# Scores of a local attention: one matmul for each head on 64 rows of TensorE, in place of one for each pair of heads on 128 rows with zeros in the keys

## What is computed

```python
HEADS, DIM_HEAD, WINDOW, QK_SCALE = 16, 64, 32, 8.0
q, k, v = split(x @ Wqkv)              # each [b, 16 heads, n, 64]
q = rotary(l2norm(q) * qs); k = rotary_inv(l2norm(k) * ksc)
# every window of 32 queries sees its own 32 keys and the 32 before them
bk2, bv2 = look(bk), look(bv)          # [b, h, windows, 64, 64]
sim = einsum('bhwie,bhwje->bhwij', bq, bk2) * QK_SCALE
sim = where(mask, -finfo.max, sim)     # it < jb, it > jb + w, or before the sequence
out = einsum('bhwij,bhwje->bhwie', softmax(sim), bv2) @ Wo
```

## Time and profile before

| | |
|---|---|
| median of 3 runs | 4558.43 us |
| the profiled execution, its own time | 4560.67 us |
| its span | 4558.9 us |
| transformer part | from about 1260 us to the end |
| PE busy over the span | 4228.4 us (93%) |
| DVE, ACT, POOL busy | 3608.9, 3009.7, 2849.6 us |
| granted TensorE clock, mean | 0.956 |

### The profile page before, as it was taken

How to read it: one execution, slowest core, us unless ns; L and a number is a source line. 1 busy time by engine, 2 the same in 40 slices (tenths; PEclk the granted TensorE clock), 3 DMA queues, 4 the chain that set the end, 5 groups by cost and what they waited for, 6 DMA issues and landing times.

```text
span 4558.9 us, 86667 instructions
## 1 busy us (share of the span) xinstructions
PE 4228.4 (93%) x32672; PEld 2902.5 (64%) x32672; DVE 3608.9 (79%) x4102; ACT 3009.7 (66%) x4797; POOL 2849.6 (63%) x1551
## 2 busy tenths in 40 slices
PE   5888889888759999999999999999999999999998
PEld 2333333333347777777877777777777777777775
DVE  3888898889867888787887888788887888878784
ACT  5655555555347777777777777777777777777774
POOL 0555455555457677676776767766676666766662
PEclk8898898988869999999999999999999999999999
DMA  1000000000010110001100010000100011000001
GB/s 37 0 0 0 0 0 0 0 0 0 19 44 22 33 31 22 22 22 33 31 22 25 19 43 22 23 23 20 45 19 25 22 33 30 19 25 22 22 22 49
DMA packets 144208, 96.47 MB, mean 21 GB/s; under 512 B 11694, under 2 KB 136624, under 8 KB 142776
## 3 DMA queue, kind: packets, MB, share of 16 engines
q1 hardware_dynamic: 143800, 90.93, 6.5%
HBM read 74.02 MB, written 16.88 MB: 20 GB/s over the span
## 4 chain that ended last, share of the span: by engine, by line
PE 68%; issue 2%; ACT 1%; POOL 1%; DVE 1%; DMA 0%; SPq 0%; ACTq 0%; POOLq 0%; DVEq 0%
PE ps L860 15%; PE ps L780 12%; PE ps L846 9%; PE ps L791 8%; PE ps L818 8%; PE ps L885 5%; PE ps L828 4%; PE ps L898 3%; PE ps L807 2%; PE ps L867 1%; PE ps L873 1%; PE ps L799 1%; PE ps L763 0%; ACT sq L950 0%; ACT w_qk L920 0%
## 5 line engine op out<-in xcount | busy, mean ns | idle before, releaser
L1269 POOL TENSOR_TENSOR resid<-resid,rnorm 128x1024 f32<-128x1024 f32 x384 | 726.8, 1903 | 537.4 <-DVE rnorm L1094 537.4
L425 POOL TENSOR_TENSOR read<-state,c_row 128x1024 f32<-128x1024 f32 x256 | 598.4, 2356 | 619.6 <-DVE state L411 494.7
L1259 POOL TENSOR_TENSOR resid<-resid,sq 128x1024 f32<-128x1024 f32 x384 | 909.0, 2372 | 101.8 <-DVE resid L1122 101.8
L860 PE MATMUL ps<-mixed,w_vo 128*128 128x128 f32 x6144 | 722.5, 276 | 4.2 <-ACT hidden L1042 2.7
L860 PEld LDWEIGHTS ps<-mixed,w_vo 128*128 128x128 f32 x6144 | 701.0, 192 | 21.6 <-issue 21.6
L780 PE MATMUL ps<-w_qk,xs_parts 128*128 128x512 f32 x2304 | 638.5, 413 | 38.9 <-DVE resid L1122 13.3
L229 PE MATMUL mamba_ps<-read,ident 128*128 128x512 f32 x1024 | 569.5, 695 | 22.4 <-DVE xc L366 19.8
L1122 DVE TENSOR_TENSOR resid<-ps,rope_l 128x1024 f32<-128x1024 f32 x384 | 467.5, 1217 | 112.9 <-ACT sq L950 109.9
L950 ACT ACTIVATE sq<-ps 128x1024 f32<-128x1024 f32 x384 | 394.3, 1027 | 239.6 <-PE ps L780 232.9
L1109 DVE TENSOR_TENSOR sq<-ps,rope_l 128x1024 f32<-128x1024 f32 x384 | 467.2, 1217 | 78.5 <-ACT sq L950 75.9
L780 PEld LDWEIGHTS ps<-w_qk,xs_parts 128*128 128x128 f32 x2304 | 417.8, 192 | 156.8 <-issue 68.2
(11 more groups left out here) (140 smaller groups left out, 6908.9 us busy)
## 6 DMA issues: line engine op xcount, KB each, us to landing
x_rows<-row_scratch SPq DMA_DIRECT2D x384, 128.0 KB, 2.8
row_scratch<-rows SPq DMA_DIRECT2D x192, 64.0 KB, 2.2
w_stage<-w_qk_hbm SPq DMA_DIRECT2D x6, 1024.0 KB, 5.9
vo_stage<-w_v_hbm SPq DMA_DIRECT2D x6, 512.0 KB, 4.0
vo_stage<-w_o_hbm SPq DMA_DIRECT2D x6, 512.0 KB, 4.8
xn<-x_hbm SPq DMA_DIRECT2D x4, 512.0 KB, 5.4
kept<-resid SPq DMA_DIRECT2D x8, 256.0 KB, 3.1
resid<-kept SPq DMA_DIRECT2D x8, 256.0 KB, 4.3
```

Of the source, the lines that this page charges most:

```text
L425: pool.tensor_tensor(read[:, u % 4, :], state[:, u % 4, :], c_row[:, (u // 2) % 2, :], ALU.mult).then_inc(read_ready, 1)
L860: last = pe.matmul(bank[:, 0:P], w_vo[:, 2 * a + h, :], mixed[:, odd, a, h, :], start=a + h == 0, stop=a == PAIRS - 1 and h == 1)
L1259: pool.tensor_tensor(qk[:, tile % 2, cols], qk[:, tile % 2, cols], sq[:, 2 + part, :], ALU.add).then_inc(done[f"rotated{part}"], 1)
L1269: pool.tensor_tensor(heads, heads, norms, ALU.mult).then_inc(done[f"normed{part}"], 1)
```

## The change

The score product is made with one matmul for each head. Head h of the pair (h = 0, 1) stands on its own 64 rows (64h to 64h + 63) in `q_t` as before and now also in `k_t`, which loses its second copy and its zeros. Each matmul has 64 rows, 32 weight columns and 64 moving columns (32 in the first window of a sequence). The first heads of all pairs go to bank S, the second ones to bank S + 1, so probabilities now stand in the order of `head_at`, and `output` picks the folded weights to match. ACT copies keys with one instruction of 128 partitions in place of two of 64. The ring has three tiles, and all four `copy_heads` wait for the score of two tiles back. The clearing of `k_t` on POOL is gone. All four order tables are new, and `copy_folded` stands ahead of the next `copy_mixed` in place of behind the last one.

```diff
-K_RING = 2
+K_RING = 3
+def head_at(place):
+    return place % PAIRS * 2 + place // PAIRS
 PE_ORDER = [
-    (3, None, "gate0"), (1, 1, "head_turn1"), (2, 2, "mix0"), (2, 1, "output"), (1, 1, "head_turn0"), (2, 2, "mix1"),
+    (2, 0, "output"), (1, 0, "row_turn"), (1, 2, "project1"), (1, 1, "head_turn3"), (1, 1, "head_turn2"), (2, 1, "mix1"),
...
-LAST_GELU = 0
+LAST_GELU = 1
...
-        mixed = [x for x in pe[:at] if x[0] in ("mix0", "mix1")][-1]
         pe.insert(at, ("fold", l))
-        insert_after(act, (mixed[0].replace("mix", "copy_mixed"), mixed[1]), ("copy_folded", l))
+        later = {(name.replace("mix", "copy_mixed"), k) for name, k in pe[at + 1:] if name in ("mix0", "mix1")}
+        act.insert(next(i for i, x in enumerate(act) if x in later), ("copy_folded", l))
...
-    k_t = sb("k_t", [P, K_RING, PAIRS, 2, P])
+    k_t = sb("k_t", [P, K_RING, PAIRS, P])
...
                 for a in range(PAIRS):
                     for w in range(WINDOWS):
-                        own = k_t[:, tile % K_RING, a, :, w * WINDOW:(w + 1) * WINDOW]
-                        to = ps[w * WINDOW:(w + 1) * WINDOW, S + a // 4, (a % 4) * P:(a % 4 + 1) * P]
...
+                        for h in range(2):
+                            rows_h = slice(64 * h, 64 * h + 64)
+                            own = k_t[rows_h, tile % K_RING, a, w * WINDOW:(w + 1) * WINDOW]
+                            first = a * 2 * WINDOW
+                            if w == 0 and t % SEQ_TILES == 0:
+                                first, keys = first + WINDOW, own
+                            elif w:
+                                keys = k_t[rows_h, tile % K_RING, a, (w - 1) * WINDOW:(w + 1) * WINDOW]
+                            else:
+                                back = k_t[rows_h, (tile - 1) % K_RING, a, P - WINDOW:P].offset
+                                keys = bass.AP(own.tensor, back, [own.ap[0], (own.offset - back, 2), (1, WINDOW)])
+                            last = pe.matmul(ps[w * WINDOW:(w + 1) * WINDOW, S + h, first:(a + 1) * 2 * WINDOW],
+                                             q_t[rows_h, odd, a, w * WINDOW:(w + 1) * WINDOW], keys, start=False, stop=True,
+                                             skip_group_check=True)
...
-                        last = pe.matmul(bank[:, 0:P], w_vo[:, 2 * a + h, :], mixed[:, odd, a, h, :],
+                        last = pe.matmul(bank[:, 0:P], w_vo[:, head_at(2 * a + h), :], mixed[:, odd, a, h, :],
...
-                    seen = 2 if c < 2 else 1
-                    if tile >= seen:
-                        after(act, ("score", tile - seen))
+                    if tile >= 2:
+                        after(act, ("score", tile - 2))
...
-                    act.copy(k_t[0:64, tile % K_RING, pairs, 0, :], bank[0:64])
-                    act.copy(k_t[64:128, tile % K_RING, pairs, 1, :], bank[64:128]).then_inc(done[name], 1)
+                    dst = q_t[:, tile % 2, pairs, :] if c < 2 else k_t[:, tile % K_RING, pairs, :]
+                    act.copy(dst, bank).then_inc(done[name], 1)
...
-            pool.memset(k_t[:, :], 0.0).then_inc(const_set, 1)
```

More of the change, by code:

```diff
@@ L474 @@
 PE_ORDER = [
[7 rows of a table removed]
-    (1, 1, "prob_turn0"), (1, 3, "row_turn"), (1, 3, "score"), (1, 1, "prob_turn1"), (2, None, "variance"),
[4 rows of a table removed]
-ACT_ORDER = [
[4 rows of a table removed]
-    (2, 3, "copy_rows"), (2, 1, "copy_probs1"), (1, 3, "round"), (3, None, "log"), (1, 0, "copy_heads3"),
-    (3, None, "rstd"), (2, 1, "copy_mixed0"), (1, 0, "copy_heads1"), (1, 1, "inverse_norm"), (1, 0, "copy_heads0"),
-    (1, 0, "copy_rows"), (1, 2, "square0"), (3, None, "round_high"), (2, 3, "exponent"), (1, 0, "copy_heads2"),
[5 rows of a table removed]
-    (2, 3, "copy_mixed0"), (1, 3, "inverse_norm"), (1, 1, "exponent")]
@@ new lines @@
+POOL_ORDER = [
+    (1, 2, "rotated1"), (2, 3, "normalise_probs"), (1, 2, "normed1"), (0, 0, "rest"), (1, 3, "rotated0"),
+    (1, 2, "normed0"), (0, 1, "rest"), (1, 3, "rotated1"), (1, 3, "normed0"), (1, 3, "normed1"),
+    (1, 0, "normalise_probs"), (0, 2, "rest"), (0, 0, "rotated0"), (0, 0, "rotated1"), (1, 1, "normalise_probs"),
+    (0, 0, "normed0"), (0, 0, "normed1"), (0, 1, "rotated0"), (1, 2, "normalise_probs"), (0, 1, "rotated1"),
+    (2, None, "scale"), (0, 1, "normed1"), (2, None, "rest_high"), (0, 3, "rest"), (0, 1, "normed0"), (0, 2, "rotated0")]
@@ L644, in transformer @@
      final_low, final_high, stored) = [z[n] for n in names]
-    CONSTS_SET = 6
+    CONSTS_SET = 5
     KEPT = 16 * CHUNKS
@@ L810, in score @@
                     for w in range(WINDOWS):
-                        own = k_t[:, tile % K_RING, a, :, w * WINDOW:(w + 1) * WINDOW]
-                        to = ps[w * WINDOW:(w + 1) * WINDOW, S + a // 4, (a % 4) * P:(a % 4 + 1) * P]
-                        if w == 0 and t % SEQ_TILES == 0:
-                            to, keys = to.rearrange("p (h k) -> p h k", h=2)[:, :, WINDOW:], own
-                        else:
-                            back = own.offset - WINDOW if w else k_t[:, (tile - 1) % K_RING, a, :, P - WINDOW:P].offset
-                            keys = bass.AP(own.tensor, back, [own.ap[0], own.ap[1], (own.offset - back, 2), (1, WINDOW)])
-                        last = pe.matmul(to, q_t[:, odd, a, w * WINDOW:(w + 1) * WINDOW], keys, start=False, stop=True,
-                                         skip_group_check=True)
+                        for h in range(2):
[12 more added lines that the diff above has]
+                                             skip_group_check=True)
                 last.then_inc(done["score"], 1)
@@ L967, in stage @@
                     bank = turn_bank(f"head_turn{c}", tile).rearrange("p (j n) -> p j n", j=4)
-                    seen = 2 if c < 2 else 1
-                    if tile >= seen:
-                        after(act, ("score", tile - seen))
+                    if tile >= 2:
+                        after(act, ("score", tile - 2))
                     pairs = slice(4 * (c % 2), 4 * (c % 2) + 4)
-                    if c < 2:
-                        act.copy(q_t[:, tile % 2, pairs, :], bank).then_inc(done[name], 1)
-                        return
-                    act.copy(k_t[0:64, tile % K_RING, pairs, 0, :], bank[0:64])
-                    act.copy(k_t[64:128, tile % K_RING, pairs, 1, :], bank[64:128]).then_inc(done[name], 1)
+                    dst = q_t[:, tile % 2, pairs, :] if c < 2 else k_t[:, tile % K_RING, pairs, :]
+                    act.copy(dst, bank).then_inc(done[name], 1)
                 return stage
```

26 lines of the change are left out of this document (13 added, 13 removed), and 45 rows, old and new, of tables (ACT_ORDER, DVE_ORDER, PE_ORDER).

## The result

Of the changed kernel four runs gave 4585.05 to 4593.66 us, median **4590.58 us**; the kernel before ran at 4558.27 to 4563.87 us, median 4560.35 us. The ratio is 1.0063, with a 95% interval of 1.0047 to 1.0079: the change makes the kernel **0.6% slower**, 30 us, where 3.1% less was forecast. The profiled execution took 4587.93 us, with a span of 4586.1 us and a mean granted clock of 0.953.

A forecast was written before the change was run, and what follows sets the result against it. PE was taken to bound the layers. From the profiled 4560.7 us, -163 (score stage) +15 (order) +6 (seam) gave 4418.7, set to 4416 us for the median of the runs, 3.1% less; range 4380 to 4485 us.

The forecast's parts named there:

- What bounds the kernel: In the layers PE is the bound with 1% idle; time taken off it comes off the run, until DVE is next.
- The score stage: PE's score matmuls: eight tiles share a slot, stage falls from 1.89 to 1.04 us, 163 us saved in all.
- the third point under it: Score stage start: 4 matmuls and 7 loads begin in 35 ns, so the array, not instruction supply, is waited for.
- rival C: Score stage: eight share a slot, but supply or loads stretch it; 1.4 us, gain 94 us, 4485 us; chance 0.12.
- Instructions: Fetching of PE's added instructions, some 98 pieces: nothing in the sum, up to 0.4 us a tile, 77 us, in the range.
- The order: New engine orders in the layers: DVE's share rises from 80% to about 85%, its queue later more often; +15 us.
- Rival D: New order makes PE wait for DVE or POOL in the layers, giving back 60 to 80 us; 4480 us; chance 0.08.
- The seam: Fold's second copy-out no longer covered before the mix: 1.2 us at each of 5 seams, +6 us; late ACT counted nothing.
- ACT, POOL and the ring: Fewer key copies (223 us of ACT), no clearing of `k_t` on POOL, third ring tile: each worth nothing by itself.
- Rivals A and B: Score matmuls: each start has its own price, 4921 us, chance 0.11; or only four run side by side, 4579 us, chance 0.05.
- The range: Whole run: 4380 to 4485 us, said to hold the first case and over half of C and D, near 0.8.
- the first case: The forecast's own case for the whole run, 4380 to 4445 us, given 0.64.

The follow-up runs named there:

- the cut stage: New score product in the old orders, each score stage split into two halves with one or two other PE stages between: 4566.0 us, ratio 1.0006.
- the product alone: Kernel before with only the new score product (one matmul per head, keys in one copy), old orders and ring of two: 4528.35 us, ratio 0.9927.
- the orders alone: Changed kernel with the score product back on 128 rows and 128 columns, keeping new orders and ring of three: 4623.34 us, ratio 1.0130.

## Why the prediction was wrong

**What bounds the kernel** was read rightly in the main: time taken off PE in the layers comes off the run, but not all of it. With half of the new product's matmuls the score stage is 1.1 us shorter than before, 211 us in all, but the run only 170 (4566.0 to 4395.79 us); 26 us are the wait for ACT's copy of the probabilities. A score stage of 1.04 us would probably have met a part of it too; no run shows how much. PE's 1% of idle time before did not tell how soon another engine would be late.

**The score stage** is the first step that failed. Right: the slot is shared by eight tiles and takes about 0.06 us, 32 matmuls long. The step that failed is the third point under it, that 4 matmuls and 7 loads in 35 ns show the array to be waited for and not the supply. They show only the start of a stage, when instructions had been got ready while PE was at the mask, as the fast start of each half of the cut stage suggests. "What no row shows is such a rate kept up" named the gap, and then the burst was taken over it. Kept up, 16 loads and matmuls take 67 ns, behind eight matmuls that take 170 ns. The stage lasts 1.41 us and not 1.04, so it gives 0.475 x 192 = 91 us and not 163: rival C, which put the gain at 94 and was given 0.12. Of the 0.37 us the pause makes 0.11, the pace of 67 ns in place of 56 makes 0.12, and the further time at some eights 0.12; the cause of this last third is open.

**Instructions.** "I put nothing in the sum, and up to 0.4 us a tile in the range": measured 33.0 us at the scores' line, 0.17 us a tile. That what is held ahead covers the burst was assumed, and did not hold in 27 of the 192 stages. Of the 91 us of shorter stages the scores keep 50 to 52, and with the losses elsewhere the product alone brings 33. Elsewhere the idle that is put down to issue rises from some 13 to 22 us with the product alone; what the rest of the 18 us outside the scores is stays open (PE's idle time there grew by 8 us only).

**The order** is the second step, "+15 us in all", where the orders cost 60 with the seam's 6 in it, so about 54. It was built on busy shares: DVE's was to go from 80% to 85%, with its idle time as a reserve. It missed two things. DVE's busy time is not a property of its instructions: moved against POOL's, the same ones took 208 us more. The row for it was there to be seen (538 ns for 32 elements a row), but it was not among the rows shown. And what counts is what stands behind a long instruction in the queue, which the order alone shows: `affine` and `refine` had each come to stand ahead of an `add_output`. Moving these two gave back some 37 of the 60 us, and guard and refinement as reductions about all of them. Rival D had the mechanism, "PE waits for DVE or POOL", at 60 to 80 us, but as a rival, beside C; both came true together, and no case in the prediction had their sum. Even that sum, 4485 + 60 to 80 = 4545 to 4565 us, would have been too low, by the stalls for instructions and the product's losses in other stages.

**The seam** was right: 6.3 us forecast at 6, ACT not late. **ACT, POOL and the ring:** the ring is worth nothing, as forecast. ACT is busy for 223 us less, as forecast; neither this nor the clearing was tried alone, and PE's wait for the first weights is as it was (27.8 us, before 27.6).

**Rivals A and B** fell. There is no price of 29.5 ns for a start: eight start in 56 to 67 ns, 7 to 8.4 ns each. The Trainium skill's floor of about 25 ns from start to start ("TensorE: Matmul & The Clock Gate", section "Back-to-back issue gap") does not hold for matmuls on different tiles; these rows decide against it.

**The sum, by measured terms:** 4560.7 - 33 (product, with its stalls) + 60 (orders and seam) = 4588, against 4587.9 in the profile. Forecast were -163 and +21. That it comes out says nothing more, since both terms are steps between the spans of three kernels, the changed one among them; a better sign is that by the medians the kernel with the orders alone gives about the same two steps, 33 and 62 us.

**The range** did not follow from its own terms either: 10 us more of idle time in each of six layers and 15 us at the seams come to about 4470 us, not 4445, and the first case with somewhat over half of C and D has about 0.75, not 0.8. The measured time lies far outside either.

## What to carry to other kernels

A burst at the start of a stage shows what was got ready before it, not a rate; where a change needs a denser stream than any stage of the trace keeps up, take the kept-up rate as unknown, and count how many instructions are used in the time in which a piece of them is brought. Before an order is judged by busy shares, look for instructions that last longer than their elements ask (here 538 ns beside 224 ns): here they stood behind another engine, and moving them changed their length. Then ask, for every long instruction of the queue, who waits for the one behind it. And where two rivals don't exclude each other, give their sum a place in the range.

## What the runs showed that was not expected

- Loads and matmuls on small tiles start at 3.7 ns each on average for the first 32 pairs of a stage with 64 columns (238 ns), then, behind eight pairs that take 170 ns, mostly at 4.2 ns, with 32 columns as with 64. Cut in two, the second half has the fast start again.
- PE stands still for 0.2 to 3.5 us inside such a stage, in some 20 to 27 of 192 stages, each time until 1.2 to 1.6 us after a piece of instructions has landed; halving the burst takes the loss from 29 to 13 us.
- A DVE instruction of 32 elements a row with both inputs in SBUF lasts until 44 to 54 ns after the POOL instruction that it began beside, up to 2.29 us for 0.19 us of work.
- The layer norm's scaling (L1177), with one tensor input, went from 587 to 1482 ns in the new orders, although it ran beside POOL in both. The traces tell the cases apart by how long POOL's instruction still had to run: the scaling takes 546 ns, or that rest and 0.28 us more, whichever is longer. This fits all 48 of them within 15 ns in each of eleven kernels. Before, the rest was 0.13 us, with `affine` moved 0.35, in the changed kernel 0.99 (or 1.8). Timeline in pairs, from the kernel before, the one with `affine` moved and the changed one:

```profile
3032.99 2.38 POOL L1259 TENSOR_TENSOR resid<-resid,sq 128x1024 f32<-128x1024 f32 x1
...
3035.24 0.55 DVE L1170 TENSOR_SCALAR xc_ff<-xc_ff,lp 128x512 f32<-128x512 f32 x1
```

```profile
2994.25 1.91 POOL L1275 TENSOR_TENSOR resid<-resid,rnorm 128x1024 f32<-128x1024 f32 x1 [0.42 <-DVE rnorm L1101]
...
2995.81 0.64 DVE L1177 TENSOR_SCALAR xc_ff<-xc_ff,lp 128x512 f32<-128x512 f32 x1
```

```profile
2991.82 1.90 POOL L1275 TENSOR_TENSOR resid<-resid,rnorm 128x1024 f32<-128x1024 f32 x1 [0.42 <-DVE rnorm L1101]
...
2992.73 1.27 DVE L1177 TENSOR_SCALAR xc_ff<-xc_ff,lp 128x512 f32<-128x512 f32 x1
```
